# Second-layer columns of a graph network: pairs of node tiles against groups of four, with 512 moving columns

## The reference, cut to what matters

```python
h = jax.nn.relu(gat_conv(x, src, dst, W1, a_src1, a_dst1, b1))
h = jax.nn.relu(gat_conv(h, src, dst, W2, a_src2, a_dst2, b2))
return h @ Wfc + bfc
```

## Time and profile before

| | us |
|---|---|
| median of 3 runs | 2237.66 |
| lowest, highest | 2236.56, 2237.82 |
| profiled execution, its own time | 2232.96 |
| its span, first to last instruction | 2231.3 |
| mean granted clock of TensorE in it | 0.995 of full |

### The profile page before, as it was taken

How to read it: one execution, slowest core, us unless ns; L and a number is a source line. 1 busy time by engine, 2 the same in 40 slices (tenths; PEclk the granted TensorE clock), 3 DMA queues, 4 the chain that set the end, 5 groups by cost and what they waited for, 6 DMA issues and landing times.

```text
span 2231.3 us, 36385 instructions
## 1 busy us (share of the span) xinstructions
PE 2194.4 (98%) x12269; PEld 1882.9 (84%) x12269; DVE 1489.0 (67%) x4615; ACT 1024.5 (46%) x2028; POOL 934.6 (42%) x931
## 2 busy tenths in 40 slices
PE   8999999999999999999999999999999999999997
PEld 6878878888899888888999999988888777888785
DVE  8777878754876856665335665267776777688675
ACT  5982112232466632222224665344444666676454
POOL 2018637745222234366542223013444554753542
PEclk9999999999999999999999999999999999999998
DMA  6434565453477657786225666357667777776431
GB/s 217 146 137 136 152 198 188 166 149 107 158 253 248 243 172 273 266 272 238 79 89 191 212 235 243 114 179 241 209 224 236 253 252 247 248 258 234 160 124 67
DMA packets 192559, 435.82 MB, mean 195 GB/s; under 512 B 45815, under 2 KB 74686, under 8 KB 191838
## 3 DMA queue, kind: packets, MB, share of 16 engines
q1 hardware_dynamic: 127034, 249.08, 32.3%
q0 software_dynamic: 65360, 184.67, 26.3%
HBM read 242.68 MB, written 190.96 MB: 194 GB/s over the span
## 4 chain that ended last, share of the span: by engine, by line
PE 73%; DVE 2%; ACT 1%; DMA 1%; issue 1%; POOL 0%; POOLq 0%; SPq 0%; ACTq 0%; DVEq 0%
PE held_ps L2769 6%; PE held_ps L2771 5%; PE held_ps L2770 5%; PE held_ps L2726 5%; PE held_ps L2744 4%; PE held_ps L2728 4%; PE held_ps L2727 4%; PE held_ps L2745 4%; PE held_ps L2746 4%; PE g_t_ps L86 4%; PE g_h_ps L2726 2%; PE g_h_ps L2744 2%; PE g_h_ps L2728 2%; PE g_h_ps L2727 2%; PE g_h_ps L2745 2%; PE g_h_ps L2746 2%
## 5 line engine op out<-in xcount | busy, mean ns | idle before, releaser
L2864 ACT ACTIVATE g_act_t<-g_t_ps,held_b_col 128x256 f32<-128x256 f32 (+1 forms) x480 | 198.9, 467 | 361.8 <-PE g_t_ps L86 361.8
L720 DVE CUSTOM_DVE_ANT_0 g_prod<-g_h_sb,g_a_rows 128x256 f32<-128x256 f32 x632 | 224.2, 419 | 75.7 <-ACT g_h_sb L587 69.2
L2769 PE MATMUL held_ps<-fc_w_hi,g_x_hi 128*128 128x512 f32 x632 | 267.9, 424 | 2.1 <-DVE g_x_lo L3041 2.0
L3039 DVE CAST g_x_hi<-g_act_t 128x512 fp32r<-128x512 f32 (+1 forms) x240 | 103.3, 430 | 216.5 <-ACT g_act_t L2864 216.0
L2771 PE MATMUL held_ps<-fc_w_hi,g_x_lo 128*128 128x512 f32 x632 | 247.3, 391 | 0.0
L2770 PE MATMUL held_ps<-fc_w_lo,g_x_hi 128*128 128x512 f32 x632 | 246.7, 390 | 0.0
L484 PE MATMUL g_h_ps<-g_w_hi,g_x_hi 128*128 128x512 f32 x616 | 242.5, 394 | 3.8 <-DVE g_x_lo L706 2.0
L485 PE MATMUL g_h_ps<-g_w_lo,g_x_hi 128*128 128x512 f32 x616 | 241.2, 392 | 0.0
L486 PE MATMUL g_h_ps<-g_w_hi,g_x_lo 128*128 128x512 f32 x616 | 240.9, 391 | 0.0
L2744 PE MATMUL held_ps<-g_x_hi,held_w_hi 128*128 128x256 f32 x768 | 222.7, 290 | 1.3 <-DVE g_x_lo L3041 1.3
L2746 PE MATMUL held_ps<-g_x_hi,held_w_lo 128*128 128x256 f32 x768 | 217.2, 283 | 0.0
(11 more groups left out here) (446 smaller groups left out, 5724.8 us busy)
## 6 DMA issues: line engine op xcount, KB each, us to landing
h<-g_h_sb SPq DMA_DIRECT2D x120, 512.0 KB, 4.4
h<-g_rows_own SPq DMA_DIRECT2D x40, 512.0 KB, 4.9
g_x_in<-in_dram SPq DMA_DIRECT2D x39, 512.0 KB, 4.0
h_cols<-g_h_sb SPq DMA_DIRECT2D x38, 512.0 KB, 4.1
xb_rows<-in_dram SPq DMA_DIRECT2D x19, 1024.0 KB, 5.6
xb<-xb_rows SPq DMA_DIRECT2D x19, 1024.0 KB, 4.4
g_x_in<-h_cols SPq DMA_DIRECT2D x38, 512.0 KB, 6.1
g_x_in<-h SPq DMA_DIRECT2D x21, 512.0 KB, 5.3
```

Source lines behind the costliest of these rows:

```text
L2769: pe.matmul(out, xh, fc_hi[:, k, :], start=(k == 0), stop=False)
```

## The change

The twelve macros 26 to 37 become six quads (`QUADS` = 26, 28, ..., 36), each of four tiles and eight halves. In a quad's half f, block column f of W2 stands and the 512 nodes of four tiles move: 24 matmuls of 512 (`quad_columns`). `quad_hi` and `quad_lo` lie where the two buffers of `x_hi` and `x_lo` lay, so a quad has one buffer: block k of the next quad is rounded when PE has used block k in the last half of this one (`slot_free`). The rounding moves from DVE's cast to ACT's copy (`round_quad`), in `roundings(h)` ahead of `evac(h)`; DVE only subtracts (`split_quad`, in `rests(h)`). PE waits for each block by itself in the first half of a quad. The relu waits in `act_t` and `a_rows` (`quad_act`) meanwhile.

A quad is filled in eight portions of one block of four tiles, in halves 2 to 5 of the quad before (quad 26: in halves 101 to 103; macro 38: halves 148 and 149). All four tiles must have landed for the first portion, and `gather(q + 2)`, `gather(q + 3)` are issued together at POOL's first half of q. Macro 38 is split at half 151, in one go. The edge sums are put at other halves (`beside_quads`), still from 119 to 147. `h2_cols` holds a quad in rows of four tiles, so its loads for the Wfc product come in pieces of 1 KB where they were 4 KB.

```diff
@@ -2033,9 +2033,13 @@
     at1 = {SUMS1 + paced(t): t for t in range(ET)}
-    at2 = {SUMS2 + paced(t): t for t in range(ET)}
-    src_ahead = {-4: 0, -3: 1, -1: 2, 0: 3, **{paced(t) + 1: t + 4 for t in range(ET - 4)}}
-    own_ahead = {paced(t) - 1: t for t in range(ET)}
+    beside_quads = lambda t: 8 * (t // 5) + (0, 1, 3, 4, 6)[t % 5] if t < 15 else 9 + t
+    at2 = {SUMS2 + beside_quads(t): t for t in range(ET)}
+    src_ahead, own_ahead = {}, {}
+    for start, pace in ((SUMS1, paced), (SUMS2, beside_quads)):
...
+        src_ahead[start] = {-4: 0, -3: 1, -1: 2, 0: 3, **{pace(t) + 1: t + 4 for t in range(ET - 4)}}
+        own_ahead[start] = {pace(t) - 1: t for t in range(ET)}
@@ -2106,6 +2114,14 @@
             return [(k, f) for i, k, f in ((2, 2, 0), (2, 6, 1), (3, 2, 2), (3, 6, 3)) if i == h]
+        if m == QUADS[0] - 1:
+            return [(k, f) for i, k, f in ((1, 2, 0), (1, 6, 1), (2, 0, 2), (2, 3, 3), (2, 6, 4), (3, 0, 5), (3, 3, 6), (3, 6, 7))
+                    if first_half[m] + i == h]
+        if quad_of(m) is not None:
+            q = quad_of(m)
+            last = q == QUADS[-1]
+            return [(k, f) for f in range(FILLS if last else KC) for i, k in ((2 + f // 2 + 2 * last, 2 + f % 2 * 4),)
+                    if first_half[q] + i == h]
@@ -2123,6 +2139,37 @@
+    QUADS = range(ENDS // 2 + 6, GM - 2, 2)
...
+    def quad_of(m):
+        return m // 2 * 2 if m // 2 * 2 in QUADS else None
+    quad_places = [(tiles(q)[0] - ENDS) // 2 for q in QUADS]
...
+    def target(h):
+        q = quad_of(halves_of[h][0])
+        return halves_of[h][0] + 1 if q is None else q + 2
+    def roundings(h):
+        if h == first_half[QUADS[0]] - 2:
+            return [(QUADS[0], k) for k in range(KC // 2)]
+        if h == first_half[QUADS[0]] - 1:
+            return [(QUADS[0], k) for k in range(KC // 2, KC)]
+        return [(q, k) for q in QUADS[1:] if h == first_half[q] - 1 for k in range(KC)]
+    def rests(h):
+        if h == first_half[QUADS[0]] - 1:
+            return [(QUADS[0], k) for k in range(KC // 2)]
+        if h == first_half[QUADS[0]]:
+            return [(QUADS[0], k) for k in range(KC // 2, KC)]
+        return [(q, k) for q in QUADS[1:] if h == first_half[q] - 1 for k in range(KC)]
@@ -2141,9 +2188,13 @@
         hi_at = sb.end
+        act_end = sb.end
...
         tile_end = sb.end
+        quad_hi = Space(nc, "g2", act_end)("quad_hi", [P, KC, 2 * G], F32R)
+        quad_lo = Space(nc, "g2", act_end + 4 * KC * 2 * G)("quad_lo", [P, KC, 2 * G], F32R)
@@ -2365,6 +2417,20 @@
+        def quad_act(k):
+            rows = act_t[:, :, :].rearrange("p k g -> p (k g)") if k < KC // 2 else a_rows[:, :, :].rearrange("p a c -> p (a c)")
+            return rows[:, k % (KC // 2) * 2 * G:(k % (KC // 2) + 1) * 2 * G]
+        def slot_wait(engine, q, k):
+            if q == QUADS[0]:
+                engine.wait_ge(tile_done, halves_done(q - 2 + k // (KC // 2)))
+            elif k == KC - 1:
+                engine.wait_ge(tile_done, halves_done(q - 1))
+            else:
+                engine.wait_ge(slot_free, (KC - 1) * QUADS.index(q - 2) + k + 1)
@@ -2402,9 +2468,15 @@
                     sp.wait_ge(evac_done, 2 * u + 2)
-                    place = (columns_of(u // 2)[:, u % 2 * HC:(u % 2 + 1) * HC] if makes_columns(u // 2) else
-                             rows_of_tile(order[u]))
-                    sp.dma_start(place, h_sb[u % 3][:, :]).then_inc(h_stored[u % 3], 16)
+                    q = quad_of(u // 2)
+                    if q is not None:
+                        at = (tiles(q)[0] - ENDS) // 2
+                        place = quad_rows(at)[:, (u - 2 * q) * HC:(u - 2 * q + 1) * HC]
+                        sp.dma_start(place, h_sb[u % 3][:, :]).then_inc(h_stored[u % 3], 16)
+                    else:
+                        place = (columns_of(u // 2)[:, u % 2 * HC:(u % 2 + 1) * HC] if makes_columns(u // 2) else
+                                 rows_of_tile(order[u]))
+                        sp.dma_start(place, h_sb[u % 3][:, :]).then_inc(h_stored[u % 3], 16)
@@ -2448,8 +2520,14 @@
                     for j, t in enumerate(tiles(m)):
-                        rows = columns_of(m)[:, j * HC:(j + 1) * HC] if takes_columns(m) else rows_of_tile(t)
-                        sp.dma_start(x_in[s][j][:, :], rows).then_inc(h_loaded[s][j], 16)
+                        at = (tiles(m)[0] - ENDS) // 2
+                        if takes_columns(m) and at // 2 * 2 in quad_places:
+                            rows = quad_rows(at // 2 * 2).rearrange("p (k a g) -> p k a g", k=KC, a=2)
+                            sp.dma_start(x_in[s][j][:, :].rearrange("p (k g) -> p k g", g=G),
+                                         rows[:, KC // 2 * j:KC // 2 * (j + 1), at % 2, :]).then_inc(h_loaded[s][j], 16)
+                        else:
+                            rows = columns_of(m)[:, j * HC:(j + 1) * HC] if takes_columns(m) else rows_of_tile(t)
+                            sp.dma_start(x_in[s][j][:, :], rows).then_inc(h_loaded[s][j], 16)
@@ -2539,7 +2617,8 @@
                     s = m % 2
-                    pool.wait_ge(filled, FILLS * (m - 1))
+                    before = quad_of(m - 2)
+                    pool.wait_ge(filled, FILLS * (m - 1 if before is None else before + 2))
                     if m == A_TILES // 2 + EARLY_B // 2:
@@ -2568,16 +2647,17 @@
                         pool.wait_ge(xb_stored, 16 * XB_GROUPS)
+                        pool.wait_ge(lo_done, FILLS * (QUADS[-1] + 2))
@@ -2628,8 +2708,11 @@
                     m, j, n = halves_of[h]
-                    if h == first_half[m] and FIRST < m + 2 < MACROS and by_pool(m + 2):
+                    if h == first_half[m] and FIRST < m + 2 < MACROS and by_pool(m + 2) and quad_of(m) is None:
                         gather(m + 2)
+                    if h == first_half[m] and m in QUADS:
+                        gather(m + 2)
+                        gather(m + 3)
@@ -2690,9 +2773,25 @@
+                def fill_quad(q, k):
+                    i = turned_before(q) + k
+                    if k == 0:
+                        for m in (q, q + 1):
+                            for j in range(2):
+                                pe.wait_ge(x_loaded[m % 2][j], 16 * loads(m, j))
+                    pe.wait_ge(relu_done, i - 1)
+                    for a in range(2):
+                        for j in range(2):
+                            last = turn_whole(pe, t_ps[k % 2][:, a, j * P:(j + 1) * P],
+                                              x_in[a][j][:, k * P:(k + 1) * P], ident_r[:, :])
+                    last.then_inc(filled, 1)
...
                     if takes_columns(m):
+                        return
+                    if quad_of(m) is not None:
+                        fill_quad(m, f)
@@ -2710,11 +2809,14 @@
                     m, j, n = halves_of[h]
-                    if h == first_half[m] and m:
+                    if h == first_half[m] and m and quad_of(m) is None:
...
                         pe.wait_ge(evac_done, h - 2)
+                    if quad_of(m) is not None:
+                        quad_columns(h, quad_of(m))
+                        return
@@ -2731,6 +2833,25 @@
+                def quad_columns(h, q):
+                    f = h - first_half[q]
+                    out, part = h_ps[h % 3][:, :], slice(f * P, (f + 1) * P)
+                    for k in range(KC):
+                        if f == 0:
+                            pe.wait_ge(lo_done, FILLS * q + k + 1)
+                        xh, xl = quad_hi[:, k, :], quad_lo[:, k, :]
+                        wh, wl = w_hi[:, k, part], w_lo[:, k, part]
+                        pe.matmul(out, wh, xh, start=(k == 0), stop=False)
+                        pe.matmul(out, wh, xl, start=False, stop=False)
+                        last = pe.matmul(out, wl, xh, start=False, stop=(k == KC - 1))
+                        if k == KC - 1:
+                            last.then_inc(tile_done, 1)
+                        elif f == KC - 1:
+                            last.then_inc(slot_free, 1)
+                        for after, fill_n in fills(h):
+                            if k == after:
+                                fill(target(h), fill_n)
@@ -2850,8 +2971,26 @@
+                def relu_quad(q, k):
+                    act.wait_ge(filled, turned_before(q) + k + 1)
+                    if q == QUADS[0]:
+                        act.wait_ge(lo_done, FILLS * q)
+                        act.wait_ge(al_done, 8 * len(WITH_EDGES))
+                    else:
+                        act.wait_ge(lo_done, FILLS * (q - 2) + k + 1)
+                    act.activation(quad_act(k), t_ps[k % 2][:, :, :].rearrange("p c g -> p (c g)"), ACT.Relu,
+                                   bias=b_col[:, 0, k:k + 1]).then_inc(relu_done, 1)
+                def round_quad(q, k):
+                    slot_wait(act, q, k)
```

(66 more changed lines are left out.)

## The result

| | before | after |
|---|---|---|
| median of the runs, taken side by side, us | 2236.56 | 2251.11 |
| lowest, highest | 2231.09, 2237.82 | 2248.04, 2258.40 |
| profiled execution, its own time | 2232.96 | 2248.04 |
| its span | 2231.3 | 2246.3 |
| mean granted clock | 0.995 | 0.991 |

The ratio after to before is 1.0076 (95% interval 1.0064 to 1.0087): slower, and 6.6 us above the upper end of the range.

A forecast was written before the change was run, and what follows sets the result against it. PE, busy 98% of the span, was taken as the bound. The terms -13.4 + 4.0 + 6.3 + 2.0 = -1.1 us (gain, two waits, clock) gave 2236.6 us, range 2230.5 to 2244.5.

The forecast's parts named there:

- The gain: Macros 25 to 37: wide matmuls of 512 columns replacing two of 256 shorten PE's stream by 13.4 us, 12 to 14.
- Wait 1: Half 114: PE waits for the gathered tiles ahead of quad 30's fill, 4.0 us, 3.1 to 7.9.
- The four gathers go out at 7.4, 8.9, 10.1 and 11.4: POOL's gathers for quad 30: issue times in us behind the end of half 111, in steps of 1.49 and 0.94 + 0.30.
- T: The end of half 111, at 1153.49 us, from which the times of quad 30's gathers are counted.
- Gathers of quads 28, 32, 34, 36 priced at 0: POOL's gathers for these quads come early enough that PE doesn't wait: 0 us, bound 0 to 2.
- Over 17 us ahead of the first fill: Quads 32 to 36: POOL reaches their gathers this early, so even four issues and a landing of 9.4 us just fit.
- Wait 2: Ahead of half 152: PE waits for DVE's splits of macro 38, which stand behind rest_fc(0): 6.3 us, 5.9 to 6.6.
- The clock: The granted clock may fall to 0.50 in PE's waits, 0 to 3.35 us each; 2.0 in all, one fall behind half 152's.
- Work beside PE, 1 KB loads: Shifted DVE and ACT work costs nothing by itself; smaller load pieces for the Wfc product stay hidden: 0, 0 to 1 us.
- C: Slower: edge work delays the next quad's rounding and subtraction, each of five boundaries loses 1.0 to 1.5 us; 2242.6, chance 0.12.
- E: Slower: the quad's wide form isn't faster than the narrow one, gain 0, +12.3 us, 2250.0; chance 0.05.
- D: Slower: gathers land in 9.4 us and the clock falls long at both forecast waits, +7.5 us, 2245.2; chance 0.08.

The follow-up runs named there:

- the fast version: The changed kernel with the gathers for quads 30 to 36 two halves earlier and macro 38's splits ahead of rest_fc(0): 2219.3 us, ratio 0.9935.
- the hold taken away: The changed kernel with DVE's two scans made to start only after POOL has issued its four gathers for quad 30: 2244.63 us, ratio 1.0053.

## Why the prediction was wrong, step by step

**The gain** (13.4, bounds 12 to 14): right in mechanism and nearly in size. Measured 12.4, the difference between the fast version with wide and with narrow matmuls. Halves took 5.44 and 6.26, as forecast; 0.4 of the missing 1.0 is PE's one wait for the edge sums' evacuation by ACT (a step of 0.67 at 1207.42 in the fast version), the rest I didn't trace. The Trainium skill's 2.5 ns for a matmul ("TensorE: Matmul & The Clock Gate", Part 1) doesn't hold for this stream; the narrow form cost 12.4 us for 1152 matmuls, 11 ns each.

**Wait 1** (4.0, bounds 3.1 to 7.9): place right, size wrong, 10.2. The step that failed is "The four gathers go out at 7.4, 8.9, 10.1 and 11.4": POOL's price for the third and fourth, taken as 0.94 each, was 5.92 and 5.20 us. POOL was even earlier than I counted: turn_top stood at 1152.52 and the first gather at 1158.04, T + 5.5, as the trip through HBM was shorter. But the third and fourth fell beside DVE's scans. I had taken their price from rows whose two gathers ended at 1163.0, just when the first scan began at 1162.84. I read POOL's timeline alone and left out what DVE does beside it. With the hold taken away the wait was 2.4, below my lower bound since POOL was early.

**Gathers of quads 28, 32, 34, 36 priced at 0** (0 to 2): wrong for 32, which cost 5.7, and right for the others. "Over 17 us ahead of the first fill" was false: POOL reaches them behind an edge gather that waits for `split_src` on DVE and then stands 5.36 us, so the first goes out 7.9 us ahead. Without the 6.4 us of the two long edge gathers it would still have been some 14, not 17. The landing of 9.4 was within what I had allowed.

**Wait 2** (6.3): right, 6.4, with the chain as described. ACT evacuates at 1428.51, rounds Wfc at 1429.10, rest_fc stands at 1429.75, PE goes on at 1434.75.

**The clock** (2.0, one fall): three falls, 6.1 us. Two of them belong to waits that I had too short or at 0, and a working stretch lost an estimated 2.3 at most, within the bound of 3.35 for each.

**Work beside PE, 1 KB loads** (0 to 1): right. The loads of the columns now land in 7.0 us against 6.1, and between the same two matmuls of the last stage lie 601.1 us (1473.81 to 2074.89) against 601.4 (1458.55 to 2059.94).

**Rivals.** C (late hand-over of a quad) and E (no gain of pace) didn't come: no wait on `quad_lo` from quad to quad. D had the right sign and clock but too small a wait. The sum with measured terms: -12.4 + 10.2 + 5.7 + 6.4 + 6.1 = +16.0, and the distance says +15.6. Against the forecast of -1.1, wait 1 was 6.2 too small, the gathers priced at 0 were 5.7, the clock 4.1, and the gain 1.0 too large.

The hold could have been read before. Two timelines of the kernel before, POOL and DVE, show it where the keys are cut:

```profile
1095.66 3.24 POOL L1057 DMA_INDIRECT g_al_src<-al,held_tabs  x1 [0.30 <-issue]
1099.21 0.94 POOL L1058 DMA_INDIRECT g_al_dst<-al,held_tabs  x1 [0.30 <-issue]
```
```profile
1094.45 2.81 DVE L1182 TENSOR_TENSOR g_cut<-g_keys 4x2561 f32<-4x2561 f32 x1
1097.29 1.49 DVE L1184 TENSOR_SCALAR g_cut<-g_cut 4x2561 f32<-4x2561 f32 x1
```

One gather of 3.24 among dozens of 0.94, ending at 1098.90, 0.12 behind the second of DVE's long instructions. The Trainium skill has the rule that I missed and that spoke against the change ("SBUF — State Buffer", Who interferes with whom, and the summary): a DVE instruction with two inputs in SBUF contends with a GpSimd one that reads SBUF, and one blocks the other until it has finished. By that rule the scans stop the gathers beside them if issuing a gather reads SBUF (its index lies there), and the trace agrees (5.92 and 5.20 us). The same section infers that subtractions don't stop the making of a DMA's descriptors; the 4.14 and 5.36 us above speak against that, and the measurement decides. The rule is for one instruction; here a run of eight, 0.60 us each, kept POOL out to the end.

## What to carry to other kernels

An issue on POOL has a price only together with what DVE runs beside it: look at both timelines for each gather that is moved or added, and at the maximum of a group of gathers, not its median. Where a wait can be avoided by place alone, put the gathers ahead of whatever on their queue waits for another engine; here two moves of a few lines turned 0.76% slower into 0.65% faster. A wait of PE costs more than its length when the clock falls in it (here an estimated 6.1 us on top of 22.3), so a change that shortens PE's stream should be checked for each buffer that has lost its depth.
